# Text rows gathered one batch at a time, powers of the eigenvalues in the states' buffer, router weights split inside the first iteration

## The reference, cut to what matters

```
h   = concat(edges(x), (U * s @ Vt)[x_txt])          # U is 25000 x 64; x_txt holds 128 ids for each batch
h  += local attention(LN(h))                         # 16 heads, a band of 128 keys
h  += where(top 288 of 384 rows, gelu(LN(h) @ w_block), LN(h))
h  += state space(LN(h))                             # a recurrence, diagonal after a Fourier transform
h  += shared FFN(LN(h)) + 2 of 8 experts(LN(h))      # router: LN(h) @ router_w.T, softmax, top 2
```

## Time and profile before

| | |
|---|---|
| median of 3 runs | 2071.47 us (2069.86 to 2071.95) |
| the profiled execution | 2072.98 us, its span 2071.2 us |
| PE, DVE, ACT, POOL busy, share of the span | 93%, 66%, 51%, 38% |
| mean granted clock of PE | 0.977 of full speed |
| setup, turns 0 and 1 | about 0 to 235 us |
| turns 2 to 17 | about 235 to 1440 us |
| experts | about 1440 to 2071 us |

### The profile page before, as it was taken

How to read it: one execution, slowest core, us unless ns; L and a number is a source line. 1 busy time by engine, 2 the same in 40 slices (tenths; PEclk the granted TensorE clock), 3 DMA queues, 4 the chain that set the end, 5 groups by cost and what they waited for, 6 DMA issues and landing times.

```text
span 2071.2 us, 45656 instructions
## 1 busy us (share of the span) xinstructions
PE 1918.9 (93%) x14039; PEld 1626.8 (79%) x14120; DVE 1358.2 (66%) x3782; ACT 1066.4 (51%) x2510; POOL 782.1 (38%) x1269
## 2 busy tenths in 40 slices
PE   3679999999999999999999999888999999999997
PEld 3456777777777777777777777667999999999997
DVE  4657676777777777777777767654665565555653
ACT  0346455555555554555655655541664554655643
POOL 4012333343243233332432432324454454545544
PEclk8789999999999999999999999999999999999999
DMA  4320220211202212112122021111532232323222
GB/s 133 82 53 26 62 55 23 69 43 41 69 23 61 59 32 54 52 32 69 32 52 67 24 61 38 24 57 36 164 89 45 41 89 46 85 44 89 46 44 40
DMA packets 81092, 116.58 MB, mean 56 GB/s; under 512 B 20964, under 2 KB 61508, under 8 KB 78724
## 3 DMA queue, kind: packets, MB, share of 16 engines
q1 hardware_dynamic: 54372, 84.16, 15.1%
q0 software_dynamic: 23360, 27.91, 8.0%
q10 hardware_dynamic: 3312, 3.94, 0.6%
HBM read 51.58 MB, written 26.71 MB: 38 GB/s over the span
## 4 chain that ended last, share of the span: by engine, by line
PE 63%; issue 12%; DVE 11%; POOL 9%; ACT 2%; DMA 1%; POOLq 1%; ACTq 1%; DVEq 0%
PE ps L1956 14%; PE ps L1764 7%; PE ps L1968 5%; PE ps L1969 5%; PE ps L1967 5%; PE ps L1635 4%; POOL slot_rows L695 4%; PE ps L1607 3%; PE ps L1692 3%; PE ps L1712 2%; PE ps L1684 2%; PE ps L1754 2%; PE ps L1815 2%; PE ps L1777 2%; PE ps L1749 2%
## 5 line engine op out<-in xcount | busy, mean ns | idle before, releaser
L838 ACT ACTIVATE prob<-ps,mx 128x256 f32<-128x256 f32 (+1 forms) x768 | 294.3, 441 | 204.3 <-DVE mx L1194 198.6
L957 ACT ACTIVATE hid_hi<-ps,b 128x256 fp32r<-128x256 f32 x408 | 203.4, 499 | 286.3 <-PE ps L1956 286.3
L1194 DVE TENSOR_REDUCE mx<-ps 128x2 f32<-128x512 f32 (+1 forms) x384 | 227.6, 597 | 161.9 <-PE ps L1684 140.4
L1537 DVE TENSOR_TENSOR hid_lo<-hid_full,hid_hi 128x256 fp32r<-128x256 f32 x408 | 171.5, 425 | 145.7 <-ACT hid_full L960 142.0
L830 ACT ACTIVATE pT<-ps 128x512 f32<-128x512 f32 (+1 forms) x384 | 202.0, 531 | 120.3 <-PE ps L1692 79.4
L751 POOL DMA_INDIRECT result<-yb,idx_o x102 | 177.2, 1737 | 172.5 <-DVE yb L1554 150.7
L1967 PE MATMUL ps<-w_hi,hid_hi 128*128 128x256 f32 x816 | 233.5, 286 | 0.0
L1969 PE MATMUL ps<-w_hi,hid_lo 128*128 128x256 f32 x816 | 229.4, 281 | 0.0
L1968 PE MATMUL ps<-w_lo,hid_hi 128*128 128x256 f32 x816 | 229.3, 281 | 0.0
L1692 PE MATMUL ps<-ident,prob 128*128 128x128 f32 x1280 | 208.3, 277 | 6.2 <-ACT prob L838 6.0
L1684 PE MATMUL ps<-ks,qs 96*128 96x512 f32 (+1 forms) x384 | 201.3, 524 | 4.2 <-ACT prob L838 4.2
(11 more groups left out here) (310 smaller groups left out, 4244.0 us busy)
## 6 DMA issues: line engine op xcount, KB each, us to landing
w_raw<-in_w SPq DMA_DIRECT2D x16, 1024.0 KB
xin<-in_x SPq DMA_DIRECT2D x32, 384.0 KB
ks<-k_hi SPq DMA_DIRECT2D x256, 48.0 KB, 2.1
qs<-q_hi SPq DMA_DIRECT2D x120, 96.0 KB, 2.2
ks<-k_lo SPq DMA_DIRECT2D x128, 48.0 KB, 2.1
xn_rows<-xc SPq DMA_DIRECT2D x16, 384.0 KB, 2.5
result<-h SPq DMA_DIRECT2D x16, 384.0 KB
qs<-q_lo SPq DMA_DIRECT2D x60, 96.0 KB, 2.2
```

What stands on the lines that cost most here:

```text
L838: ins = act.activation(prob[:, s % PB, hh, w], ps[:, s % 2, hh * 2 * P + w.start:(hh + 1) * 2 * P], ACT.Exp, bias=mx[:, s % 2, hh:hh + 1])
L957: act.activation(hid_hi[:, f], ps[:, f % 4, 0:CHUNK], ACT.Gelu_apprx_tanh, bias=b1[half][:, f:f + 1])
L1194: dve.tensor_reduce(mx[:, s % 2], sc, AX_X, ALU.max, negate=True).then_inc(max_done.sem, 1)
```

## The change

POOL gathers the text rows of batch b + 2 inside turn b, for b = 0 to 13, into one buffer `u_rows`; batch 1's gather stands ahead of `residual(0)`. Because b is a register in the loop, the ids of the batch are first copied to a column `id_col` with a wait of POOL on its own copy. The new `gather_text` waits until ACT has copied the rows of the batch before (`ub_ready`). It stands behind `dispatch(b - 2)` and ahead of `chain_deviations(b - 1, 1)`. ACT waits for its own batch's gather in `text_rows`; its wait for all gathers ahead of turn 0 is gone. POOL's loop is one turn shorter, and turn 14 is written out.

`powers` keeps its intermediates in `st`, and DVE's wait for the stacking DMAs in turn 0 is gone. `split_router` moves to s = 15 of turn 0, ahead of `split_shared`, with the wait for `late_loaded`; `shared_split` is now raised by `split_shared`.

```diff
-        u_all = sb("u_all", [P, NB, R])
+        id_col = sb("id_col", [P, 1], I32)
+        u_rows = sb("u_rows", [P, R])
...
-            def gather_text(b, done):
-                pool.indirect_dma_start(u_all[:, b, :], None, t["U"],
-                                        bass.IndirectOffsetOnAxis(ids[:, b:b + 1], axis=0)
-                                        ).then_inc(done.sem, 16)
+            def gather_text(b):
+                pool.wait_ge(ub_ready.sem, ub_ready.at(b - 1, 1))
+                pool.tensor_copy(id_col[:], ids[:, bass.ds(b, 1)]).then_inc(id_ready.sem, 1)
+                pool.wait_ge(id_ready.sem, id_ready.at(b - 1, 1))
+                pool.sem_inc(pool_go.sem, 1)
+                pool.indirect_dma_start(u_rows[:], None, t["U"], bass.IndirectOffsetOnAxis(id_col[:, 0:1], axis=0)
+                                        ).then_inc(u_gathered.sem, 16)
...
                 if late and att:
                     dispatch(b - 2)
+                if ahead:
+                    gather_text(b + 2)
                 if chain:
                     if att:
                         chain_deviations(b - 1, 1)
...
-            for b in range(1, NB):
-                gather_text(b, u_gathered)
+            gather_text(1)
             residual(0)
...
-                act.activation(ub[:, 0:R], u_all[:, bass.ds(b, 1), :], ACT.Copy).then_inc(ub_ready.sem, 1)
+                act.wait_ge(u_gathered.sem, u_gathered.at(b, 16))
+                act.activation(ub[:, 0:R], u_rows[:], ACT.Copy).then_inc(ub_ready.sem, 1)
...
-            act.wait_ge(u_gathered.sem, u_gathered.at(0, 16 * (NB - 1)))
             sequence(0, True, False, False, True, first=True)
...
-                dve.tensor_scalar(rot[:, 0, 0:m], turn[:, 0, 0:m], re, None, ALU.mult)
-                dve.tensor_scalar(rot[:, 1, 0:m], turn[:, 0, 0:m], im, None, ALU.mult)
+                dve.tensor_scalar(st[:, 0, 0:m], turn[:, 0, 0:m], re, None, ALU.mult)
+                dve.tensor_scalar(st[:, 1, 0:m], turn[:, 0, 0:m], im, None, ALU.mult)
...
                     if first and s == 1:
                         eigenvalues()
-                        for pair in range(PAIRS):
-                            dve.wait_ge(stacked[pair].sem, stacked[pair].at(b, stacked[pair].per))
...
                     if first and s == CONV:
+                        split_router()
                         split_shared()
...
             sequence(0, True, False, False, True, True, first=True)
-            dve.wait_ge(late_loaded.sem, late_loaded.at(0, NLATE))
-            split_router()
             sequence(1, True, False, True, True, True)
```

More of the change, by code:

```diff
@@ L292, in build @@
         ids_loaded = dma_signal("ids_loaded", 0)
-        u_first = dma_signal("first_u_gathered", 0)
-        u_gathered = dma_signal("u_gathered", 0)
+        u_gathered = dma_signal("u_gathered", 16)
+        id_ready = signal("text_id_ready", 1)
         ub_zeroed = signal("ub_zeroed", 0)
@@ L605, in _ @@
         def _(pool):
-            def gather_text(b, done):
-                pool.indirect_dma_start(u_all[:, b, :], None, t["U"],
-                                        bass.IndirectOffsetOnAxis(ids[:, b:b + 1], axis=0)
-                                        ).then_inc(done.sem, 16)
+            def gather_text(b):
[5 more added lines that the diff above has]
+                                        ).then_inc(u_gathered.sem, 16)
             pool.wait_ge(ids_loaded.sem, ids_loaded.at(0, 16))
-            gather_text(0, u_first)
+            pool.indirect_dma_start(u_rows[:], None, t["U"], bass.IndirectOffsetOnAxis(ids[:, 0:1], axis=0)
+                                    ).then_inc(u_gathered.sem, 16)
             pool.wait_ge(band_ready.sem, band_ready.at(0, 1))
@@ L698, in dispatch, with sequence @@
                 pool.sem_inc(pay_free.sem, 1)
-            def sequence(b, att, late, chain, head):
+            def sequence(b, att, late, chain, head, ahead):
                 if late and att:
                     dispatch(b - 2)
+                if ahead:
+                    gather_text(b + 2)
                 if chain:
@@ L718, in sequence @@
                     residual(b + 1)
-            for b in range(1, NB):
-                gather_text(b, u_gathered)
+            gather_text(1)
             residual(0)
             pool.wait_ge(slots_cleared.sem, slots_cleared.at(0, 48))
-            sequence(0, True, False, False, True)
+            sequence(0, True, False, False, True, True)
             pool.wait_ge(late_loaded.sem, late_loaded.at(0, NLATE))
[L726 to L731, removed]
+            sequence(1, True, False, True, True, True)
+            with pool.Fori(2, NB - 2) as b:
+                sequence(b, True, True, True, True, True)
+            sequence(NB - 2, True, True, True, True, False)
+            sequence(NB - 1, True, True, True, False, False)
+            sequence(NB, False, True, True, False, False)
+            sequence(NB + 1, False, True, False, False, False)
             def gather_rows(j, n):
@@ L1054, in powers @@
                 dve.scalar_tensor_tensor(out=turn[:, 0, n:n + m], in0=turn[:, 1, 0:m], scalar=nim,
-                                         in1=rot[:, 0, 0:m], op0=ALU.mult, op1=ALU.add)
+                                         in1=st[:, 0, 0:m], op0=ALU.mult, op1=ALU.add)
                 link(dve.scalar_tensor_tensor(out=turn[:, 1, n:n + m], in0=turn[:, 1, 0:m], scalar=re,
-                                                   in1=rot[:, 1, 0:m], op0=ALU.mult, op1=ALU.add), setup_step, 0)
+                                                   in1=st[:, 1, 0:m], op0=ALU.mult, op1=ALU.add), setup_step, 0)
                 dve.tensor_scalar(im, den, 2.0, None, ALU.mult)
@@ L1142, in split_shared @@
                 dve.wait_ge(sw1_rounded.sem, sw1_rounded.at(0, 1))
-                dve.tensor_tensor(sw1_lo[:], sw1, sw1_hi[:], ALU.subtract)
+                dve.tensor_tensor(sw1_lo[:], sw1, sw1_hi[:], ALU.subtract).then_inc(shared_split.sem, 1)
             def split_router():
+                dve.wait_ge(late_loaded.sem, late_loaded.at(0, NLATE))
                 link(dve.tensor_copy(rw_hi, rw[:]), setup_step, 0)
-                dve.tensor_tensor(rw_lo, rw[:], rw_hi, ALU.subtract).then_inc(shared_split.sem, 1)
+                dve.tensor_tensor(rw_lo, rw[:], rw_hi, ALU.subtract)
             def turned_rests(b):
```

1 line of the change is left out of this document (removed).

## The result

The changed kernel takes 2083.03 us (median of five runs, 2080.66 to 2089.07), the kernel before 2071.95 beside it (median of five, 2069.86 to 2074.09). The ratio is 1.0058, 95% interval 1.0039 to 1.0076: slower by 11 us, where 18.5 were forecast. The profiled execution is the slowest of the five, 2089.07, with a span of 2087.3; against before's 2071.2 it is 16.1 us longer.

What follows compares the result with a forecast made beforehand. PE, busy 93%, was taken to bound the kernel, with POOL's queue from dispatch to deviations on each turn's path. Terms 25.8 + 14.4 - 12.5 - 8.2 - 0.3 + 0.3 = +19.5 us gave 2090 us, range 2071 to 2106.

Steps and rivals of the forecast that it cites:

- Gather inside a turn: POOL's queue between slot writes' landing and deviations: 2.15 us a turn, 25.8 us for twelve turns.
- The upper bound of 3.0 us a turn: Gather's price in a turn if its issue takes 1.68 us, as a slot write has; 36 us for twelve.
- the Trainium skill's rule: During certain fast DVE modes POOL cannot write DMA descriptors; each gather could take 1.68 us, +8 us on the sum.
- What the longer wait does to the clock: PE's 3.1 us wait at the transposes drops its clock: 9 falls in 12 turns at 1.6 us, 14.4 us.
- the bound of 19: Upper bound of the clock term in the loop: 12 falls at 1.6 us each.
- No train of gathers in the setup: Setup standstill before ACT's copy to xT, taken to come from POOL's gathers, goes: -12.5 us; other bound 0.
- rival 2: The setup's standstill isn't the gathers', so its 12.5 us gain is missing: 2103 us, chance 0.16.
- No stacking wait in turn 0: DVE's row maximum of unit 1 no longer waits 8.25 us for stacking DMAs: -8.2 us, bounds -6 and -8.25.
- router split: DVE's two instructions leave the path before turn 1, -0.3 us; they come ahead of split_shared in turn 0, +0.3 us.

Runs made afterwards that it cites:

- two experiments: Changed kernel with the gather issued behind POOL's shared_residual (2042.26 us, ratio 0.9919), and the changed kernel again, unchanged (2084.83 us, ratio 1.0129).
- the repeated run: The changed kernel again, unchanged, beside the kernel before: 2084.83 us against 2058.7, ratio 1.0129.
- the three groups of the experiments: Twelve follow-up runs in three groups, each on its own chip; the kernel before takes 2058 to 2059 us in all three.

## Why the prediction was right in its sign, and where its sum was off

Slower was forecast with 0.76, 2090 us with a range of 2071 to 2106; it is slower, at 2083. By the steps:

- *Gather inside a turn*: right in mechanism and size. 2.15 us a turn forecast, 2.09 by PE's wait in the first trace (3.02 - 0.93), 2.05 between two experiments, and nothing with the gather moved. The upper bound of 3.0 us a turn is 2.8 by its own terms (0.18 + 0.81 + 1.68 + 0.16). It didn't come into play, nor did the Trainium skill's rule (SBUF — State Buffer, "The 'DVE blocks DMA' trap"): the fifteen gathers take 1.00 to 1.04 us each. Beside the twelve of the loop DVE ran a row maximum of 0.69 us and at most the start of a sum, so these runs don't test that rule.
- *What the longer wait does to the clock*: right in kind, too small. The step took 9 falls in 12 turns, 14.4 us; in the profiled execution it was every one of the twelve, at 1.4 us each, and in two turns the fall was longer and followed by one more, 3.2 us more each. From the twelve turns' +47.5 less 25.1 of wait 22.4 us are left for it, and that is what this term measured, net of the one fall that the kernel before has in these turns (1.6 us). The Trainium skill (TensorE: Matmul & The Clock Gate, "HAM oscillation — how this bites in real kernels") tells of a loop whose wait for data makes the clock drop in every pass; the trace agrees in that, with twelve falls in twelve turns, and the repeated run nearly, with eleven. I had no row that spoke for nine, and 22.4 lies above the bound of 19, which had no room for the second falls.
- *No train of gathers in the setup*: the size was right in that pair of measurements (the 12.5 are gone, 11.2 of them at the copy), the cause is not shown. The step inferred it from "nothing else was running". Trains of gathers stand in six traces of the experiments without any standstill. The removed train can be what mattered in the first measurement, or the changed kernel may have missed the standstill for another reason; this stays open. In this term the forecast was lucky: where there is no standstill, the term is 0 and the change costs 26 us. That is near rival 2, which had 31.5: right in the three groups of the experiments, wrong in the pair that was forecast.
- *No stacking wait in turn 0* and *router split*: -8.2 forecast together, -6.8 measured alone up to turn 2; the 3.3 us that came later had no term. In the first pair it was -10.5 beside the copy's 11.2, more than the two edits give alone. Where the kernel before had the standstill, its clock was also at the lower level from 38.7 to 55.8 us, and its turn 2 began 14.5 us later than without, 1.9 more than its copy.
- A term was missing: -10 us in the experts, from the address of buffers that the change doesn't name. The prediction costed operations and waits, and had no term for a buffer's size. That omission and the clock's undersized term nearly cancel (-9.6 and +8.0), and so the total came close; that too is luck.

Sum with what was measured: 25.1 for the waits, 22.4 for the clock, -11.2 and -10.5 up to turn 2, -0.1 in turns 14 and 15, -9.6 in the experts: 16.1, the difference of the two spans. The median of five is 6 us below the profiled execution, and the fastest, 2080.66, ran at a mean granted clock of 0.976 where the profiled one had 0.971: the +11 of the medians has less clock loss in it than this trace.

## What to carry to other kernels

An indirect gather of one buffer costs its queue the copy, the gap and the issue, 2.1 us here; put it where that engine idles, not between a landing and the work that others wait for: moved down a few calls in one queue it turned the same change from 1.3% slower into 0.8% faster (0.5% of that are the 32 bytes below). A pause of 3 us on PE in an otherwise full turn costs more by the clock behind it (2.1 us of wait, 1.4 of clock), so a wait that grows must be priced with it, in every turn; the clock fell in twelve and in eleven of twelve such turns. And when a buffer's size changes, compare the start addresses of what PE streams against multiples of 64 bytes, before and after: an unused 32 bytes gave 0.5%.

## What the runs showed of the hardware that I had not expected

- Second-layer matmuls (128x256, fp32r) follow each other in 117.8 ns with their buffers 32 bytes past a multiple of 64, and in 113.4 ns at a multiple, in all fourteen traces; moving the buffers by 4096 bytes changes nothing, moving them by 32 gives the 113.4. First-layer matmuls of the same shape take 120 ns either way.
- Behind a wait of 3.0 us the clock stays at its lower level for 3.4 us in most turns, behind one of 4.25 for 6.8 us in eleven turns of twelve. Two turns with such a wait, of 3.08 and 3.06 us in two runs, had no fall at all.
- The same program has a standstill of 12.5 us in its setup in one measurement and none in another: PE's transposes end at 37.46 and ACT, which waits for their signal alone, starts at 49.99; in the other they end at 37.36 and it starts at 37.40. Five runs' times speak for the standstill in the first measurement, 50 of 51 against it on three chips. What causes it is open.
